# A preln GNN kernel: the up product of the node stage by Strassen's scheme, with sums made on GpSimd

## The reference

```python
h = jnp.maximum(_layernorm(x, axis=-1), 0.0)
x = x + segment_sum((h @ W.T)[dst] * edge_weight[:, None], src, N)   # N = 50000 nodes, 25000 edges, D = 256
h = jnp.maximum(_layernorm(x, axis=-1), 0.0)
agg = segment_sum(h[src], dst, N)
h1 = (agg + h) @ W1 + b1                                              # 256 -> 1024
h1 = relu((h1 - mean(h1)) * rsqrt(var(h1) + 1e-5) * gamma + beta)     # mean, var over the nodes
out = x + relu(h1 @ W2 + b2)                                          # 1024 -> 256
```

## Time and profile before

| | |
|---|---|
| time, median of 3 runs | 3891.73 us (3891.07 to 3893.2) |
| profiled execution: time, span | 3888.09 us, 3886.3 us |
| PE busy | 3434.7 us, 88% |
| PEld busy | 2911.2 us, 75% |
| DVE busy | 2267.6 us, 58% |
| ACT busy | 2163.0 us, 56% |
| POOL busy | 1039.7 us, 27% |

### The profile page before, as it was taken

How to read it: one execution, slowest core, us unless ns; L and a number is a source line. 1 busy time by engine, 2 the same in 40 slices (tenths; PEclk the granted TensorE clock), 3 DMA queues, 4 the chain that set the end, 5 groups by cost and what they waited for, 6 DMA issues and landing times.

```text
span 3886.3 us, 56828 instructions
## 1 busy us (share of the span) xinstructions
PE 3434.7 (88%) x17113; PEld 2911.2 (75%) x17113; DVE 2267.6 (58%) x5129; ACT 2163.0 (56%) x3533; POOL 1039.7 (27%) x801
## 2 busy tenths in 40 slices
...
GB/s 344 338 193 193 194 193 130 115 175 167 163 156 158 158 309 360 360 129 126 118 110 126 114 113 129 108 113 129 108 117 126 108 122 121 109 126 116 112 126 68
DMA packets 305854, 619.82 MB, mean 159 GB/s; under 512 B 34997, under 2 KB 186800, under 8 KB 299856
## 3 DMA queue, kind: packets, MB, share of 16 engines
...
...
## 4 chain that ended last, share of the span: by engine, by line
PE 59%; POOL 18%; issue 11%; ACT 6%; another core or an unknown queue 3%; DMA 2%; DVE 1%; ACTq 0%; POOLq 0%; DVEq 0%
PE ps_a L1286 28%; PE ps_b L1300 19%; PE ps_b L1301 9%; POOL x_table L552 7%; POOL agg_table L552 6%; ACT late L685 4%; POOL edge_tiles L542 3%; POOL edge_ring L542 1%; DMA x_table<-edge_tiles,scatter_now 1%; DMA agg_table<-edge_tiles,scatter_now 1%; ACT late_r L703 1%; PE ps_b L1204 1%; ACT edge_tiles L631 1%; PE ps_b L1215 0%
## 5 line engine op out<-in xcount | busy, mean ns | idle before, releaser
L1300 PE MATMUL ps_b<-w_hl,late_r 128*128 128x512 f32 x3128 | 1129.0, 396 | 0.0
L749 ACT ACTIVATE hid<-ps_a,bn_bias,bn_scale 128x512 f32<-128x512 f32 (+1 forms) x784 | 609.1, 777 | 734.6 <-PE ps_a L1286 734.6
L1129 DVE TENSOR_TENSOR late_r<-hid,late_r 128x512 fp32r<-128x512 f32 (+1 forms) x784 | 537.1, 685 | 815.2 <-ACT late_r L754 815.2
L1286 PE MATMUL ps_a<-late_r,w_hi 128*128 128x512 f32 x3136 | 983.9, 395 | 0.0
L1301 PE MATMUL ps_b<-w_hl,late_r 128*128 128x256 f32 x3128 | 876.3, 280 | 0.0
L1300 PEld LDWEIGHTS ps_b<-w_hl,late_r 128*128 128x128 f32 x3128 | 587.6, 188 | 138.9 <-issue 0.5
L1286 PEld LDWEIGHTS ps_a<-late_r,w_hi 128*128 128x128 f32 x3136 | 540.5, 188 | 108.9
L1286 PE MATMUL ps_a<-late_r,w_lo 128*128 128x512 f32 x1568 | 611.8, 390 | 0.0
L1301 PEld LDWEIGHTS ps_b<-w_hl,late_r 128*128 128x128 f32 x3128 | 590.0, 189 | 26.4
L754 ACT ACTIVATE late_r<-hid 128x512 fp32r<-128x512 f32 (+1 forms) x784 | 494.8, 631 | 71.7
L1215 PE MATMUL ps_b<-edge_tiles,edge_same 128*128 128x256 f32 x1568 | 404.1, 422 | 0.0
...
## 6 DMA issues: line engine op xcount, KB each, us to landing
x_rows<-x_table SPq DMA_DIRECT2D x291, 512.0 KB, 4.3
late<-agg_table SPq DMA_DIRECT2D x194, 512.0 KB, 5.7
...
hT_f<-hT_table SPq DMA_DIRECT2D x97, 512.0 KB, 3.6
out<-zeros SPq DMA_DIRECT2D x97, 512.0 KB, 6.7
x_table<-edge_tiles,scatter_now POOLq DMA_INDIRECT x196
```

Of the source, the lines that this page charges most:

```text
L749: act.activation(hid[m % 2][:, 0:w].rearrange("p (r a b) -> p r a b", a=BANDS, b=SQUARE), by_row, ACT.Relu, scale=bn_scale[:, m:m + 1], bi ...
L1129: dve.tensor_tensor(hid_lo[m % 4][:, 0:w], hid[m % 2][:, 0:w], hid_hi[m % 4][:, 0:w].bitcast(F32), ALU.subtract).then_inc(hid_lo_ready, 1)
L1286: ins = pe.matmul(ps_a[:, 2 + m % 2, 0:w], w_part[:, kb, cols], h_part[:, kb * w:(kb + 1) * w], start=(t == 0), stop=(t == len(terms) - 1))
L1300: pe.matmul(ps_b[:, r, :], hid_hi[m % 4][:, cols], w2, start=(m == 0), stop=(m == MB - 1), skip_group_check=True)
```

## The change

Nothing changes in the edge stages but the split of W1, and nothing in the gram stage but places in memory. In the node stage the up product of a chunk is seen as 2 x 2 blocks: W1's columns in pairs of blocks of 128 hidden units (four pairs i per chunk) by its two blocks of 128 features, and hT's two blocks of features by two halves of 256 nodes. Winograd's form of Strassen's scheme makes each pair's four blocks from seven products in place of eight. The sums of W1's blocks (S1 to S4) are made once on VectorE. The sums of h's blocks (T1 to T4) are made for each chunk on GpSimd (`mix_h`), which takes over `add_agg` too. Products that share an output block are added in PSUM; what can't be added there VectorE moves: it copies P1 to the third quarter of a pair's two banks and P5 to p5_sb (`take_p1_p5`), and makes U2 + P5 and U3 + P5 (`add_p5_to_u2`, `add_p5_to_u3`). Each product is three matmuls of 256 columns. The steps of TensorE are listed for each pair in ORDER, where a d is a piece of `down` (one group of nodes, a 512 and a 256 column matmul).

```diff
+        def quarters(i):
+
+            pair = ps_a[:, 2 * (i % 2):2 * (i % 2) + 2, :].rearrange("p t (v x) -> p (t v) x", v=2)
+            return pair
...
+
+            def store(n, s, k):
 
                 sp.wait_ge(out_ready, n + 1)
-                if load:
-                    load_main(n + LOADS, s)
-                sp.dma_start(chunk_of(out, n), tile_of(out_sb[s % 2], n)).then_inc(out_stored[s % 2], 16)
-                sp.wait_ge(out_stored[s % 2], 16 * turn_of(s, k) + 16)
+                for rows, parts, bands in band_rows(out, n):
+                    sp.dma_start(rows, out_sb[s % 2][parts, bands, :]).then_inc(out_stored[s % 2], 16)
+                if has(n, 2):
+                    load_x1_out(n + 2, s)
+                if has(n, 5):
+                    sp.wait_ge(h_ready, n + 4)
+                    load_main(n + 5, s + 5)
+                if has(n, 3):
+                    turn_h(n + 3)
+                sp.wait_ge(out_stored[s % 2], 16 * ROWS * turn_of(s, k) + moved_rows(n))
...
 
+            def add_agg(n, s, k):
+
+                p, j = shape_of(n)
+                pool.wait_ge(ln_ready, n + 1)
+                pool.wait_ge(main_loaded[s % 2], 32 * turn_of(s, k) + 32)
+                if not is_first(n):
+                    pool.wait_ge(turned_ready, n)
+                by_square = h[0].rearrange("p j d -> p (j d)").rearrange("p (c j e) -> p j c e", c=CB, e=SQUARE)
+                pool.tensor_tensor(by_square[0:p, 0:j, :, :],
+                                   relu_ln[0][0:p, 0:j, :].rearrange("p j (c e) -> p j c e", e=SQUARE),
+                                   agg_in[s % 2][0:p, 0:j, :].rearrange("p j (c e) -> p j c e", e=SQUARE), ALU.add).then_inc(h_ready, 1)
+
+            def mix_h(n):
+
+                half = width(n) // 2
+                b12, b11, b22, b21 = (hT_f[:, q * half:(q + 1) * half] for q in range(4))
+                t1, t2, t3, t4 = (t_f[:, q * half:(q + 1) * half] for q in range(4))
+                pool.wait_ge(hT_loaded, 16 * n + 16)
+                if not is_first(n):
+                    pool.wait_ge(hT_lo_ready, 2 * n)
+                pool.tensor_tensor(t1, b12, b11, ALU.subtract).then_inc(t1_ready, 1)
+                pool.tensor_tensor(t3, b22, b12, ALU.subtract)
+                pool.wait_ge(t1_ready, n + 1)
+                pool.tensor_tensor(t2, b22, t1, ALU.subtract).then_inc(t2_ready, 1)
+                pool.wait_ge(t2_ready, n + 1)
+                pool.tensor_tensor(t4, b21, t2, ALU.subtract).then_inc(t_ready, 1)
+
+            def main(n, s, k):
+                if has(n, 2):
+                    add_agg(*after_next(n, s, k))
+                if has(n, 1):
+                    mix_h(n + 1)
```

The order of nodes inside a chunk is another (bands), so the output's store and a separate load of x for `finish` (`load_x1_out`) are four transfers each, of rows of 1 KB. h, relu_ln, h_turned and hT_f are single buffers now; x and agg are loaded five chunks ahead into two slots. In the diff, `add_agg` and `mix_h` are GpSimd's; VectorE's part:

```diff
+            def take_p1_p5(n, i):
+
+                half = width(n) // 2
+                dve.wait_ge(p1_done, PAIRS * n + i + 1)
+                if i > 0 or not is_first(n):
+                    dve.wait_ge(u3_read, PAIRS * n + i)
+                dve.tensor_copy(quarters(i)[:, 2, 0:half], quarters(i)[:, 0, 0:half])
+                dve.tensor_copy(p5_sb[:, 0:half], quarters(i)[:, 1, 0:half]).then_inc(p1_p5_taken, 1)
+
+            def add_p5_to_u2(n, i):
+
+                half = width(n) // 2
+                dve.wait_ge(p1_p5_taken, PAIRS * n + i + 1)
+                dve.wait_ge(p6_done, PAIRS * n + i + 1)
+                dve.tensor_tensor(quarters(i)[:, 3, 0:half], quarters(i)[:, 2, 0:half], p5_sb[:, 0:half], ALU.add).then_inc(u2_read, 1)
+
+            def add_p5_to_u3(n, i):
+
+                half = width(n) // 2
+                dve.wait_ge(up_done, MB * n + 2 * i + 1)
+                dve.tensor_tensor(quarters(i)[:, 1, 0:half], quarters(i)[:, 2, 0:half], p5_sb[:, 0:half], ALU.add).then_inc(u3_read, 1)
+
...
-                for m in range(MB):
-                    dve.wait_ge(hid_hi_ready, MB * n + m + 1)
-                    if m >= 4 or not first:
-                        dve.wait_ge(down_done, MB * n + m - 3)
-                    dve.tensor_tensor(hid_lo[m % 4][:, 0:w], hid[m % 2][:, 0:w], hid_hi[m % 4][:, 0:w].bitcast(F32),
-                                      ALU.subtract).then_inc(hid_lo_ready, 1)
-                    if m == 0 and has(n, 1):
-                        turn_squares(*following(n, s, k))
-                    if m == 2 and not first:
-                        finish(n - 1, (s - 1) % LOADS)
-                    if m == 4 and has(n, 3):
+                for i in range(PAIRS):
+                    before = not (is_first(n) and i == 0)
+                    last = (n, 2 * i) if i else (n - 1, MB)
+                    take_p1_p5(n, i)
+                    if before:
+                        hidden_low(last[0], last[1] - 2)
+                    if i == 0 and has(n, 1):
+                        turn_squares(n + 1)
+                    if i == 1 and not is_first(n):
+                        read_down(n - 1, s - 1, 0)
+                    if i == 2 and has(n, 1):
+                        hT_low(n + 1, s + 1, False)
+                    if i == 3 and not is_first(n):
+                        finish(*preceding(n, s, k))
+                    add_p5_to_u2(n, i)
+                    if i == 1 and not is_first(n):
+                        read_down(n - 1, s - 1, 1)
+                    if before:
+                        hidden_low(last[0], last[1] - 1)
+                    add_p5_to_u3(n, i)
+                    if i == 0 and has(n, 3):
                         pick_norm(n + 3, (s + 1) % 2)
-                    if m == 6 and has(n, 1):
-                        hT_low(n + 1, s + 1)
-                    if m == 7 and has(n, 2):
-                        add_agg(*following(*following(n, s, k)))
```

TensorE's part:

```diff
-                    pe.wait_ge(down_read, 2 * n)
+            def product(n, s, i, number):
+
+                weight, part, to, first = {1: (A11, B11, 0, True), 2: (A12, B21, 0, False), 3: (S4, B22, 3, False),
+                                           4: (A22, T4, 2, False), 5: (S1, T1, 1, True), 6: (S2, T2, 2, False),
+                                           7: (S3, T3, 2, False)}[number]
+                half = width(n) // 2
+                cols = slice(part * half, (part + 1) * half)
+                terms = ((w1_hi, hT_hi), (w1_hi, hT_lo), (w1_lo, hT_hi))
+                for t, (w_part, h_part) in enumerate(terms):
+                    ins = pe.matmul(quarters(i)[:, to, 0:half], w_part[:, weight, i, :], h_part[s % 2][:, cols],
+                                    start=(first and t == 0), stop=(t == len(terms) - 1), skip_group_check=True)
+                return ins
+
+            def p5(n, s, i):
+                if i == 0:
+                    pe.wait_ge(hT_lo_ready, 2 * n + 2)
+                if i >= 2 or not is_first(n):
+                    pe.wait_ge(hid_ready, MB * n + 2 * i - 2)
+                product(n, s, i, 5)
+
+            def p1(n, s, i):
+                product(n, s, i, 1).then_inc(p1_done, 1)
+
+            def p6_p2(n, s, i):
+                pe.wait_ge(p1_p5_taken, PAIRS * n + i + 1)
+                product(n, s, i, 6).then_inc(p6_done, 1)
+                product(n, s, i, 2)
+
+            def p7_p3(n, s, i):
+                pe.wait_ge(u2_read, PAIRS * n + i + 1)
+                product(n, s, i, 7)
+                product(n, s, i, 3).then_inc(up_done, 1)
+
+            def p4(n, s, i):
+                pe.wait_ge(hid_ready, MB * n + 2 * i + 1)
+                product(n, s, i, 4).then_inc(up_done, 1)
+
...
+                    pe.wait_ge(hid_lo_ready, MB * n + m + 1)
+                if m == 0 and a % 2 == 0 and not is_first(n):
...
+                    ins.then_inc(down_done, 1)
+                elif m == MB - 1 and a == 1:
+                    ins.then_inc(down_half, 1)
+
+            def downs(n, i):
+
+                groups = {0: [(n - 1, 5), (n - 1, 6)], 1: [(n - 1, 7), (n, 0)], 2: [(n, 0), (n, 1), (n, 2)], 3: [(n, 3), (n, 4)]}[i]
+                for n_of, m in groups:
+                    if is_first(n) and m >= 5:
+                        continue
+                    for a in range(BANDS):
+                        if m == 0 and (a < 2) != (i == 1):
+                            continue
+                        yield n_of, m, a
...
+
```

400 lines of the change are left out of this document (244 added, 156 removed).

## The result

| | before | after |
|---|---|---|
| median | 3891.4 us (3888.2 to 3893.2, 4 runs) | 4162.6 us (4154.9 to 4173.3, 4 runs) |
| span of the profiled execution | 3886.3 us | 4153.1 us |
| PE busy | 88% | 84% |
| DVE busy | 58% | 72% |
| POOL busy | 27% | 40% |

The ratio is 1.070 (95% interval 1.0686 to 1.0711): slower by 271 us, where the prediction said 3957 us and at most 4050. Its direction was right, its size and range were not.

What follows compares the result with a forecast made beforehand. TensorE's instruction stream was taken to bound the node stage; 98 × (22.91 − 22.29) = +61 us, plus 2 and 3 once only, on 3888.1 gives 3954, with the median 3.6 above: 3957 us, range 3850 to 4050.

Steps and rivals of the forecast that it cites:

- What bounds the kernel; TensorE's stream: Node stage: TensorE's own instruction stream sets the pace; it falls to 21.2 us a chunk, at most −107 us in all.
- The schedule of one chunk: Node stage, four pairs: 22.11 us a chunk against 22.29, with 0.93 of the 1.1 us saved coming back as waits.
- the first rival: No mutual hold-up of GpSimd and VectorE in the node stage: 22.11 us a chunk, 3878 us; chance 0.27.
- The stop in pair 2: TensorE waits ahead of P7 for VectorE's sum behind hT_low: 0.29 us a chunk lost without hold-up.
- GpSimd's prices: GpSimd additions in the node stage: 0.68 us for 256 elements, 2.45 for 1024, estimated from MEMSET and AFFINE_SELECT.
- The hold-up of instructions with two SBUF inputs: VectorE's hidden_low, hT_low and finish wait out a running GpSimd instruction; at the mixes +0.8 us, 22.91 a chunk.
- the third rival: Small copies (pick_norm) are held inside add_agg too, pair 1 slips 0.75 us: 4031 us; chance 0.17.
- The failed step: hT_f's landing in the node stage: 3.42 + 7.5 = 11.0, plus 1 us for more transfers queued ahead: 12.0.
- the fourth rival: hT_f lands late, ScalarE waits at take_hT from 13.05; at 13.75 with the hold-up 4025 us; chance 0.10.
- The sum: 98 chunks × (22.91 − 22.29) = +61, once-only costs 2 and 3, onto 3888.1: 3954; median 3.6 above: 3957 us.
- The range: 3850 to 4050 us, leaving out what is beyond half of the second rival (shorter VectorE chain, 0.08) and the third's upper part.
- Wrong if: Node-stage signs against it: hidden_low or hT_low stay at 0.69, GpSimd's addition far from 2.4 us, ScalarE waits for hT_f.

Runs made afterwards that it cites:

- the re-timed kernel without sums: Changed kernel with turn_h first, small copies moved, U2 + P5 before hT_low in pair 2, pair 1's down and read_down reordered, GpSimd's five sums left out: 3858.9 us, 0.9914.
- the turn first alone: Changed kernel with SP's store(n) beginning with turn_h(n + 3), ahead of the output's stores and the loads, nothing left out: 4003.3 us, ratio 1.0304.

## Why the prediction was wrong, point by point

- *What bounds the kernel; TensorE's stream.* Right. The slots are 0.119 and 0.235 us, the stream without stops 21.3 us (21.2 forecast): of the 21.8 us a chunk in the re-timed kernel without sums 0.55 are stops.
- *The schedule of one chunk.* Nearly right where it was alone: without GpSimd's sums, with the copies moved and with the turn on time a chunk takes 400 × 148 / 2657 = 22.28 us against 22.11 set out, stops about 1.0 in all against 0.93, of which down_read 0.63 against 0.64. The stop in pair 2 is 0.15 and not 0.29, and one of 0.15 stands in pair 0, where the margin was set at 0.07. The ratio is 1.0022 where the first rival's mechanism gives 3878, 0.997.
- *GpSimd's prices.* 2.40 and 0.74 us against 2.45 and 0.68. The estimate from the Trainium skill, GPSIMD Engine Reference, section 3.1, was 2.25 and 0.56; the traces lie above it, by a third for 256 elements, and nearer to the figures worked out from the earlier trace rows. Those came from two instructions of another kind, so that the two errors are small is in part luck.
- *The hold-up of instructions with two SBUF inputs.* Right in mechanism and near in size: 0.68 a chunk against +0.8. The rule of the Trainium skill, SBUF — State Buffer, section "Who interferes with whom", holds in these traces (1.36 for 0.69, 1.44 for 0.74). What the same section of the Trainium skill says of copies in the two-port mode would cover the third rival's copy too, held 2.0 us (1.80 to 2.10 in 48 chunks); no trace shows in which mode it ran.
- *The third rival, the small copies* (0.17). They are held, for longer than the 0.75 us I gave it to cost; what it costs is 43 us where 74 was worked out, and nothing while the turn is late.
- *The failed step:* "I add 0 to 2 us, 1 in the middle: 12.0", hT_f's landing, and the price set on it. The load landed 10.5 us after the transpose's end on the mean, 3.0 later than the 7.5 to which 0 to 2 was added. That alone was the fourth rival (0.10), "each 0.1 us after that is 0.1 a chunk, 10 us", counted from 13.05: by that rule hT_f at 3.4 + 10.5 = 13.9 costs 0.9 us a chunk, some 85 us. With the landing brought back by 2.5 us, 153 us went, 1.6 a chunk. The rule priced ScalarE at take_hT only, and where no mixes stand behind it (87 us) it is about right. It missed that behind hT_f stand four mixes, stretched to 4.4 us, and take_mixed, where ScalarE was to be at 15.6 and now stood 1.9 us; and that hT_low and pair 3's copies queue behind it. The late finish also issues its 2 MB right against the next turn, so that the lateness may feed itself; that part is argued. I read the landing of the store from a trace in which nothing stood just ahead of it (16 us of rest in SP's queue).
- *The sum.* The kernel with the turn on time and the copies not held has 22.97 us a chunk against 22.91 forecast, and its ratio is 1.0194 where 3957 us is 1.017. In part that is luck: the schedule came out 0.17 longer than set out and the hold-up 0.12 shorter. What the sum missed is the transfer (+153) and the copies (+43), undone one after the other from 1.0698 to 1.0194.
- *The range.* I gave each rival a chance as if the others were off; here the hold-up, the held copy and the late hT_f held at once. By the prediction's own prices the three give 3957 + 74 + 68 = 4099, which is outside the range and still 64 us short of what was measured, so wider chances alone would not have held it: the late hT_f was priced too low.
- *Wrong if,* as the prediction put it, "ScalarE waits for hT_f". It does: in 20 of 48 chunks for the load itself (14.7 us in all, up to 1.3), and in all 48 for the mixes made from it (89.7).

Whether VectorE's hold-ups and the late turn lengthen each other in the kernel after, beyond the order in which I undid them, stays open: without the mixes alone 158 us go, with the turn first alone 153, and with all sums out, the copies moved and the turn first 263. The prices depend on the order: the turn is worth 153 first and 87 last.
